# FFN inputs and W1/W3 as two scaled fp16 parts, and one FFN matmul behind each context group

## What is computed

```python
xn = _layernorm(x, axis=-1)
# attention: causal softmax(q k^T / sqrt(32)) v, then Wo
s = _L0_attn_ref(xn, Wq, Wk, Wv, Wo)
# FFN
up_gate = jnp.einsum('bsd,hd->bsh', x, W1)
up_lin = jnp.einsum('bsd,hd->bsh', x, W3)
hidden = jax.nn.silu(up_gate) * up_lin
hidden = fwht(hidden)
out = jnp.einsum('bsh,dh->bsd', hidden, W2)
...
g = _silu(_L0_ffn_ref(xn, W1, W2, W3))
x = x + s * g
```

## Time and profile before

| | |
|---|---|
| median of 3 runs | 972.14 us (972.06 to 972.33) |
| the profiled execution | 972.55 us |
| its span, first to last instruction | 970.8 us |
| PE / DVE / ACT / POOL busy | 99% / 73% / 58% / 37% of the span |
| mean granted TensorE clock | 0.999 |
| stretches read below as the heads | 96 to 393 us and 555 to 853 us |

### The profile page before, as it was taken

One profiled execution on the slowest core, in us unless ns is written; L12 is line 12 of the kernel. 1 busy time (PEld: TensorE's weight loads), 2 busy tenths in 40 slices (PEclk: granted clock), 3 DMA queues, 4 the chain that ended last, 5 costly groups with the idle time before them and its releaser, 6 DMA issues. The chain is left out here.

```text
span 970.8 us, 18488 instructions
## 1 busy us (share of the span) xinstructions
PE 959.4 (99%) x6392; PEld 797.7 (82%) x6392; DVE 707.1 (73%) x1441; ACT 565.7 (58%) x1172; POOL 357.2 (37%) x587
## 2 busy tenths in 40 slices
PE   8999999999999999999999999999999999999997
PEld 7888888888888887888888888888888888878886
DVE  7777888888888887755554578888888888833343
ACT  4324777777777786623334166777777777832221
POOL 1896764656656442000001024453443543500000
PEclk9999999999999999999999999999999999999999
DMA  9793235232232405951145523233223232181111
GB/s 285 259 271 110 77 89 142 78 88 56 77 89 56 121 23 201 345 203 44 45 174 204 174 55 88 57 78 89 55 78 88 56 78 56 45 342 49 43 44 44
DMA packets 55757, 110.58 MB, mean 114 GB/s; under 512 B 5360, under 2 KB 22384, under 8 KB 55152
## 3 DMA queue, kind: packets, MB, share of 16 engines
q1 hardware_dynamic: 55664, 109.40, 37.1%
HBM read 75.56 MB, written 33.55 MB: 112 GB/s over the span
## 5 line engine op out<-in xcount | busy, mean ns | idle before, releaser
L1024 DVE TENSOR_TENSOR p_lo<-stage,p_hi 128x512 f16<-128x512 f32 (+2 forms) x288 | 188.3, 654 | 58.4 <-ACT p_hi L743 58.0
L1337 PE MATMUL f<-xt_hi,w_hi 128*128 128x512 f32 x512 | 202.0, 394 | 0.0
L1337 PE MATMUL f<-xt_hi,w_lo 128*128 128x512 f32 x512 | 201.8, 394 | 0.0
L1337 PE MATMUL f<-xt_lo,w_hi 128*128 128x512 f32 x512 | 201.5, 394 | 0.0
L733 ACT ACTIVATE stage<-s 128x512 f32<-128x512 f32 (+2 forms) x288 | 150.8, 524 | 82.9 <-PE s L1298 81.1
L743 ACT ACTIVATE p_hi<-stage 128x512 f16<-128x512 f32 (+2 forms) x288 | 158.8, 551 | 24.9 <-POOL stage L595 20.2
L1298 PE MATMUL s<-qk_st 98*128 98x512 f32 (+2 forms) x384 | 141.4, 369 | 0.0
L1011 DVE CUSTOM_DVE_ANT_0 m<-m,causal 128x1024 f32<-128x1024 f32 (+3 forms) x128 | 131.0, 1023 | 2.7 <-PE m L1282 2.7
L602 POOL TENSOR_TENSOR w_lo<-w,w_hi 128x256 fp32r<-128x256 f32 x128 | 118.3, 953 | 28.5 <-ACT w_hi L764 27.2
L595 POOL TENSOR_SCALAR_AFFINE_SELECT stage<-stage 128x128 f32<-128x128 f32 x192 | 57.4, 306 | 179.0 <-ACT stage L733 178.2
L1337 PEld LDWEIGHTS f<-xt_lo,w_hi 128*128 128x128 f32 x512 | 96.6, 189 | 18.2
(11 more groups left out here) (179 smaller groups left out, 1831.3 us busy)
## 6 DMA issues: line engine op xcount, KB each, us to landing
qk_st<-qk_parts SPq DMA_DIRECT2D x96, 256.0 KB, 4.3
w<-w1w SPq DMA_DIRECT2D x32, 512.0 KB, 3.6
qk_parts<-qk_hi SPq DMA_DIRECT2D x32, 256.0 KB, 3.2
qk_parts<-qk_lo SPq DMA_DIRECT2D x32, 256.0 KB, 4.3
wht_in<-w SPq DMA_DIRECT2D x4, 1024.0 KB, 10.9
w_butterflied<-wht_in SPq DMA_DIRECT2D x4, 1024.0 KB, 5.9
w_transformed<-g_hi SPq DMA_DIRECT2D x8, 512.0 KB, 3.2
w_transformed<-g_lo SPq DMA_DIRECT2D x8, 512.0 KB, 4.7
```

Source lines behind the costliest of these rows:

```text
L1024: dve.tensor_tensor(p_lo[s][:], expd[q % NE][:, 0:end - need], p_hi[s][:], ALU.subtract).then_inc(p_lo_done, 1)
L1337: mm = pe.matmul(F[m][:, 0, :], w, v, start=k == 0, stop=k == GMM - 1)
```

## The change

The FFN's operands become fp16 pairs. `xt` is kept for Q, K and V; beside it ACT and DVE make `x16_hi` and `x16_lo` of the same PSUM tile, times 2048 (one instruction each, eight tiles per batch, placed by `X16_AFTER`). A transpose that uses the bank again, and in batch 0 the bound of V, wait for them.

W1/W3 get a power-of-two scale per tile, the same for all rows. In batch 0 ACT squares each raw tile with a sum per row (`w13_squares`: four tiles in `project`, twelve at slot 5 of heads 0 to 11), for which SP loads all tiles but the first once more (`scan_w13`). PE adds the sums over the rows by a product with ones (`sum_of_squares`, six in all), DVE makes scale, half and unscale of it (`scale_of_w13`, five small instructions). ACT applies the scale while rounding to fp16. POOL multiplies the fp32 tile by it, in two instructions of 512 columns among the four pieces, in all heads but the first of a batch, where ACT does it. tanh and `hide` take the scale out again.

PE keeps one FFN matmul of a slot with a context group and runs it behind the group.

SBUF tiles are laid out anew: `p_hi` and `p_lo` share the room of `xt`.

```diff
+ONES_AFTER = [3, 4, 5]
+X_TOP = 2048.0
-W13_AT = 2
+SQUARES_AT, W13_AT = 5, 2
+X16_AFTER = {2: (0,), 3: (1,), 4: (2, 3), 7: (6, 7), 8: (4,), 9: (5,)}
+SCAN_AFTER = {10: (1,), 13: (2, 3)}
+SQUARES_AFTER = {8: (0,), 13: (1,)}
+SQUARES_OF_V = {4: (2,), 5: (3,)}
+SCAN_FIRST, SCAN_GROUP = 4, 3
...
+            def scan_w13(t):
+                if t > SCAN_FIRST:
+                    sp.wait_ge(w13_sum, t)
+                elif t == 1:
+                    sp.wait_ge(split_lo, NQ)
+                elif t == 2:
+                    sp.wait_ge(wv_lo_done, KT)
+                sp.dma_start(scan_tile(t), w1w3[t]).then_inc(scan_in[t % 3], 16)
...
                         load_stack(sp, n + 2)
+                        if b == 0 and j + SCAN_FIRST < NH:
+                            scan_w13(j + SCAN_FIRST)
                         load_w13(n + 2)
...
-                pool.tensor_tensor(w13_lo[n % 2][at], w13[at], w13_hi[n % 2][at].bitcast(F32), ALU.subtract
+                if piece % 2 == 0 and n % NH > 0:
+                    pool.tensor_scalar(w13[:, piece // 2, :], w13[:, piece // 2, :], w13_scale[:, n % NH:n % NH + 1],
+                                       None, ALU.mult).then_inc(w13_scaled, 1)
+                pool.wait_ge(w13_scaled, 2 * n + piece // 2 + 1)
+                pool.tensor_tensor(w13_lo[n % 2][at], w13[at], w13_hi[n % 2][at], ALU.subtract
                                    ).then_inc(w13_lo_done, 1)
...
+            def x16(b, t):
+                act.wait_ge(xt_lo_done, b * NT + t + 1)
+                act.activation(x16_hi[:, :, t * P:(t + 1) * P], xt_bank(t).rearrange("p (k c) -> p k c", k=KT),
+                               ACT.Copy, scale=X_TOP).then_inc(x16_hi_done, 1)
...
+                    if t == 1:
+                        scale_first(b * NH)
+                        w13_high(b * NH)
...
+                act.activation(scan_tile(n) if n else w13_hi[0][:], scan_tile(n), ACT.Square,
+                               accum_out=w13_ssq[:, n:n + 1]).then_inc(w13_sum, 1)
...
+                    if b == 0 and s == SQUARES_AT and j + SCAN_FIRST < NH:
+                        w13_squares(j + SCAN_FIRST)
                     if s == W13_AT and j + 1 < NH:
                         w13_high(n0 + j + 1)
...
-                dve.tensor_tensor(hidden_part(n, c), hidden_part(n, c), F[1][:], ALU.mult
-                                  ).then_inc(hidden_done, 1)
+                after(dve, w13_scale_step, scale_steps(n) if n < NH else 0)
+                dve.scalar_tensor_tensor(hidden_part(n, c), hidden_part(n, c), w13_unscale[:, n % NH:n % NH + 1],
+                                         F[1][:], ALU.mult, ALU.mult).then_inc(hidden_done, 1)
...
                 if t >= 4:
-                    pe.wait_ge(xt_lo_done, b * NT + t - 3)
+                    pe.wait_ge(x16_lo_done, x16_no(b, t - 4))
...
                 pe.wait_ge(xt_lo_done, NT)
+                pe.wait_ge(x16_lo_done, x16_no(0, 6))
...
+            def sum_of_squares(n):
+
+                pe.wait_ge(w13_sum, scan_groups[n][-1] + 1)
+                pe.matmul(w13_sum_bank(n), ones_r[:].bitcast(F32), w13_ssq[:, tiles_of(n)], start=True, stop=True
+                          ).then_inc(w13_sum_ps, 1)
...
-                    v = (xt_hi, xt_lo, xt_hi)[p][:, kt, c * W:(c + 1) * W]
+                    v = (x16_hi, x16_lo, x16_hi)[p][:, kt, c * W:(c + 1) * W]
...
+                    kept = 1 if g in CTX_PLAN and g < SLOTS else 0
+                    some_ffn(at, ffn_upto(g) - kept)
...
                     if g in MT_PLAN:
                         transpose_maxima(n0 + MT_PLAN[g])
+                        if b == 0 and MT_PLAN[g] - 1 in SUM_PLAN:
+                            sum_of_squares(SUM_PLAN[MT_PLAN[g] - 1])
+                    some_ffn(ffn_upto(g) - kept, ffn_upto(g))
```

More of the change, by code:

```diff
@@ L129, in build @@
         w13 = sb("w13", [P, 2, D], F32)
-        stage = [sb(f"stage{i}", [P, D], F32) for i in range(3)]
+        stages = sb("stages", [P, 3, D], F32)
+        stage = [stages[:, i, :] for i in range(3)]
         stats = sb("stats", [P, NT, 6], F32)
@@ L151, in build @@
         with ExitStack() as r:
[L152 to L156, removed]
+            widths = [min(W, (c + 1) * W - k * P) for c, k in STEPS]
+            with ExitStack() as q:
+                xt_hi = sb("xt_hi", [P, KT, S], F32R, q)
+                xt_lo = sb("xt_lo", [P, KT, S], F32R, q)
+            p_hi = [sb(f"p_hi{s}", [P, widths[s]], F16, r) for s in range(NS)]
+            p_lo = [sb(f"p_lo{s}", [P, widths[s]], F16, r) for s in range(NS)]
+            sb("room_after_p", [P, 4 * KT * S - 2 * sum(widths)], F16, r)
+            w13_hi0 = sb("w13_hi0", [P, 2, D], F16, r)
+            w13_lo0 = sb("w13_lo0", [P, 2, D], F16, r)
             mx = [sb(f"mx{i}", [P, NT], F32, r) for i in range(2)]
@@ L254, in split_no @@
             return b * NQ + i
-        raw = [*(t[:] for t in stage), w13[:, 0, :], w13[:, 1, :]]
+        raw = [*stage, w13[:, 0, :], w13[:, 1, :]]
         def weights_loaded(b, i):
@@ L423, in project @@
                         step(slab)
+                    if b == 0:
+                        for t in SCAN_AFTER.get(g, ()):
+                            scan_w13(t)
                     if g == KT:
@@ L714, in project @@
                             split_wv(b, kt)
-                    if g == 2 * KT:
-                        w13_high(b * NH)
+                    for t in X16_AFTER.get(g, ()):
+                        x16(b, t)
+                    if b == 0:
+                        for t in SQUARES_AFTER.get(g, ()):
+                            w13_squares(t)
                 if b == 0:
@@ L724, in project, with scale_first @@
                                    ACT.Copy).then_inc(proj_hi_done, 1)
+                    if t == 1:
+                        scale_first(b * NH)
+                        w13_high(b * NH)
+                    if b == 0:
+                        for tile in SQUARES_OF_V.get(t, ()):
+                            w13_squares(tile)
                     if t == MT_BEFORE - 1:
                         maxima_hi(b * NH)
+            def scale_first(n):
+                act.wait_ge(w13_in, (n + 1) * 16)
+                act.wait_ge(w13_scale_step, scale_steps(0))
+                for m in range(2):
+                    act.activation(w13[:, m, :], w13[:, m, :], ACT.Copy, scale=w13_scale[:, 0:1]).then_inc(w13_scaled, 1)
             def exp(q):
@@ L1250, in project @@
                         transpose_v_scale()
+                    if b == 0 and g == NQK:
+                        pe.wait_ge(proj_lo_done, NQK - 1)
+                        sum_of_squares(0)
                 for r in range(FIRST_MAX_AT.count(None)):
@@ L1279, in maxima @@
                     after(pe, max_done, n * NT + r - 1)
+                if r == 1 and n == 0:
+                    pe.wait_ge(w13_scale_step, 1)
+                if r == 1 and n - 2 in SUM_PLAN:
+                    pe.wait_ge(w13_scale_step, 5 * SUM_PLAN[n - 2] + 1)
                 bank, parts = max_parts(t) if t else (X[:, 0, 0:2 * P], [(0, 2 * P)])
```

107 lines of the change are left out of this document (90 added, 17 removed).

## The result

The changed kernel takes 1009.73 us (median of four runs, 1005.17 to 1016.39) against 972.24 for the kernel before beside it: 3.8% slower, ratio 1.0381, interval 1.0358 to 1.0404. The forecast was 951.4 with a range of 940 to 962, so it missed in sign.

The account below looks back on a forecast made before the run. PE was taken as the bound, with DVE and ACT close behind. 972.55 - 25.3 - 7.3 + 1.2 + 2.7 + 6.0 + 2.0 = 951.85, then 0.41 lower for the median: 951.4 us, range 940 to 962.

Parts of the forecast that it names:

- Term 6: POOL's two multiplies among the w13_lo pieces in 30 heads, 0.6 us each: +2.0 us (0 to 6).
- rival D: POOL's multiply takes 1.9 us; scores 0 and FFN 0 of each head wait 1.9: 1000 us, chance 0.04.
- B: Rival: POOL and the DMA queue behind it hold every head's end: 970.4 us, or 958; chance 0.17.
- Term 1: 1536 FFN matmuls in fp16, 216 ns apart instead of 232.5: -25.3 us (-8.4 to -30).
- Term 2: One FFN matmul behind each context group hides the scores' fp32r load, 0.078 us for 94 groups: -7.3 us.
- Term 3: The scale's six products with ones on PE, 0.2 us each: +1.2 us.
- Term 4: x16 in the first projection: DVE's added subtractions make PE wait in batch 0, +2.7 us (0 to 5).
- Term 5: ACT's squares in 12 heads of batch 0 delay the rows of maxima for scores 0: +6.0 us (0 to 12).
- At nothing: Unscale in hide, tanh's scale, scale_first in the V groups and 15 scanned tiles of 512 KB: no cost.

Follow-up runs that it names:

- e1: The changed kernel with POOL's 60 multiplies of 128x512 left out (w13 stays unscaled for w13_lo); 974.7 us, ratio 1.002 to the kernel before.
- f4: e2 with the FFN matmul in front of the context group again, none kept behind it; 978.4 us, ratio 1.005 to the kernel before.
- f3: e2 with ACT's squares moved from step 5 to step 10, sums two tiles at a time one head later; 960.4 us, ratio 0.987.
- e2: The changed kernel with POOL's multiplies put on DVE at step 4 of a head; 974.9 us, ratio 1.002 to the kernel before.
- f1: e2 without ACT's squares in heads 0 to 11 of batch 0, their loads kept, sums preset; 965.6 us, ratio 0.992 to the kernel before.
- k1: The changed kernel with the weights' scale fixed at 1 and without POOL's slab steps in batch 0's heads; 951.2 us, ratio 0.978.
- k2: The changed kernel with scale fixed at 1, POOL's second slab step of a head waiting for p_lo of step 10; 951.6 us, ratio 0.978.
- e3: The kernel before plus only POOL's 64 multiplies of 128x512 by a column of ones, all else fp32r; 1029.3 us, ratio 1.057.

## Why the prediction was wrong, point by point

**Term 6 is the step that failed.** I took 0.6 us for POOL's multiply because a memset and a select were "nearer", both with one input or none. The nearest row was the two-input add of the same size, type and engine, 1.41 us, which I had named as the upper bound; measured is 1.56 alone and 1.85 in the mean with the waits for p_lo, above that bound. The mechanism was worked out under rival D (1.9 us a multiply, scores 0 and FFN 0 of each head late, 1000 us, chance 0.04), and in batch 1 the waits came as written: 18.8 us a head against 17.25, 1.5 where D had 1.9. That D's 1000 is near 1009.7 is in part luck: it had 57 us for the multiplies where they cost 35, and the other terms made up the difference. Term 6 is +35 us (after against e1), not +2. The rule of the Trainium skill weighed there ("GPSIMD Engine Reference", Engine selection: one-input operations near VectorE's rate) is not what the runs show for this one, 1.56 against 0.48 us, and the measurement decides. The range's upper end, 962, also left out all of D and the far half of B though one unmeasured price decided between them. (In B, half of 27 gives 957, not 958.)

**Term 1, FFN in fp16: right in the interval, too large in the sum.** 216 ns is what the rows show in a run of such matmuls. But each return from an fp32r matmul costs 11 to 12 ns, some twelve times a head. A steady head of batch 1 with fp16 and no kept matmul (f4) takes 17.41 us against 18.03: 0.62 us by 32 heads is -20 us, not -25.3.

**Term 2, the kept matmul: right mechanism, two thirds of the size.** 0.15 us a head, some -4.7 us instead of -7.3: the group with the transpose behind it gains nothing.

**Term 3, products with ones: right.** In f3 such a product moves the next FFN matmul by 0.144 us; six make 0.9 against 1.2. What I had not seen is that the five small operations behind it are 0.6 us on DVE, and where they push a p_lo behind a slab step PE loses 0.67 us.

**Term 4, x16: right.** The first scores stand at 90.39 instead of 87.52, +2.9 against +2.7 (the profiled executions of kernels with x16 lie between 88.4 and 90.8, those without between 87.1 and 87.5), and PE waits where forecast, before the bound of V (PE's timeline, to be set beside the earlier trace rows):

```profile
42.71 1.17 PE L1411 MATMUL m<-w_lo,ones_r 128*128 128x512 f32 x4 [1.34 <-DVE x_lo L1062]
```

**Term 5, squares: the place right, the wait wrong, the size half.** +12.4 us in the profiled heads of batch 0 (e2 against f1; 9.3 by the medians) and not +6.0. The wait forecast, for the rows of maxima, is 0.2 us in all in batch 0 of e2, where POOL's multiplies are gone. What PE waited for was `hidden` (8.5 us in 10 waits, of which 6.1 stay without the squares in f1) and the one load of 8.2 us with the clock's fall behind it (7.1), which I had put at nothing ("most of them in a stretch with a DMA share of 0.35"): a mean share says nothing of the one head in which a slab is loaded.

**At nothing.** The prediction had no term for POOL's slab steps. The change moved p_lo of 128x256 from just ahead of one to just behind it: the kernel before has no such collision, f1 has 11, a shift of some 0.1 us in the order. (The collisions of p_lo of 128x384, 1.27 us, are in both and cost nothing.) Of f1's 278.7 us, 9.1 are above batch 1's, 0.9 of them term 3's, and k1 and k2 show that without these collisions batch 0 is as short as batch 1. What moved the order in the changed kernel was not taken apart; e3, in fp32r, has the 11 collisions too.

The sum with measured terms: 972.2 - 20 - 4.7 + 0.9 + 2.9 + 12.4 + 8.2 + 35 = 1006.9, against 1009.7; the rest was not followed up, the four runs lie 11 us apart, and the terms mix medians and profiled executions (by the latter the 35 is 30.5). With terms 1, 2 and 4 alone it is 950.4, and k2 measures 951.6. That the forecast was 951.4 as well is chance: its gains were 8 us too large, and the 8 us of terms 5 and 6 are what k2 doesn't have.

## What to carry to other kernels

When one price that the trace doesn't show stands between a gain and a loss, take the row nearest in operand count, type and engine, and let the range hold both ends; better, measure the price alone in the kernel before, as e3 did. On a bound engine with its followers close behind, ask of each added instruction on a helper engine who waits for the end of its list, the DMA queue behind it included. And look at pairs: where VectorE's operation on two SBUF tiles and POOL's overlap, the later one waits for nearly all that is left of the other, and here a semaphore wait that put the long one second cost nothing.

## What was not expected of the hardware

- POOL multiplies 128x512 fp32 in SBUF in 1.56 us at best by a factor from a tile and in 1.49 by an immediate (means 1.79 and 1.71 in the kernel before); 256 columns take 0.92. VectorE takes 0.48 us for 512.
- VectorE's p_lo of 128x256 takes 0.42 us or 1.55, by whether it starts ahead of POOL's instruction or together with it. Its operations that read PSUM are not touched (`hidden` 0.68 and 0.67 us).
- An fp16 matmul of 512 columns costs 216 ns, but 227 directly after an fp32r one. Between fp16 and fp32r there is no gap, though the record shows the second starting 28 ns behind the first.
- The loads of 512 KB for the squares land in 6.0 us (median), but in 8.2 us behind a slab's transfers on the same queue, and with ACT waiting for it a head of 17.3 us takes 24.4.
- 2.7 us of that are the clock: after 4.3 us without a matmul the granted clock was at the 1.2 GHz level for 6.8 us, and FFN matmuls started 0.43 us apart.
